# Expert slots filled by indirect gathers of stored token rows instead of one-hot products, with the shared products reordered

## The reference: what is computed

```python
x  = x + attn0(layernorm(x)) + ffn0(layernorm(x))      # 1024 tokens of 256
xn = layernorm(x)
x  = x + attn1(xn) + moe(xn)                           # attn1: 16 heads of 16, 4 key heads

def moe(x):                                            # E=32 experts, K=4, F=176, FS=704, CAP=32
    probs = softmax(x @ Wr)
    topw, topi = top_k(probs, 4); topw = topw / sum(topw)
    shared = silu(x @ Wsg) * (x @ Wsu) @ Wsd * sigmoid(x @ Wse)
    pos = number of earlier picks of the same expert   # valid if pos < CAP
    xe[sel, pos] += x[tok] * valid                     # 32 experts x 32 slots
    ye = (silu(xe @ Wg) * (xe @ Wu)) @ Wd
    return shared + sum over picks of ye[sel, pos] * w * valid
```

## Time and profile before

| what | value |
|---|---|
| median of 3 runs | 457.9 us (457.85 to 458.16) |
| the profiled execution | 458.18 us, of which 456.4 us are its span |
| TensorE busy | 439.0 us (96%) |
| VectorE busy | 301.4 us (66%) |
| ScalarE busy | 238.6 us (52%) |
| GpSimd busy | 157.5 us (35%) |
| granted clock of TensorE | 1.00 |

### The profile page before, as it was taken

How to read it: one execution, slowest core, us unless ns; L and a number is a source line. 1 busy time by engine, 2 the same in 40 slices (tenths; PEclk the granted TensorE clock), 3 DMA queues, 4 the chain that set the end, 5 groups by cost and what they waited for, 6 DMA issues and landing times.

```text
span 456.4 us, 8792 instructions
## 1 busy us (share of the span) xinstructions
PE 439.0 (96%) x3062; PEld 387.8 (85%) x3062; DVE 301.4 (66%) x889; ACT 238.6 (52%) x656; POOL 157.5 (35%) x286
## 2 busy tenths in 40 slices
PE   2999999999999999999999999999998999999997
PEld 1788888899999999999999999999986746568897
DVE  5735576678787878787877766486889952554111
ACT  3464561786868787878676883333161233242000
POOL 3050001545455555555555301011651289500000
PEclk9999999999999999999999999999999999999999
DMA  6910011401010101010000000000999099900011
GB/s 193 233 58 2 1 47 47 157 30 47 2 47 1 47 3 46 1 50 0 1 2 2 0 1 2 1 0 1 309 276 298 6 252 296 275 4 1 0 47 46
DMA packets 40442, 32.35 MB, mean 71 GB/s; under 512 B 6432, under 2 KB 38864, under 8 KB 40400
## 3 DMA queue, kind: packets, MB, share of 16 engines
q1 hardware_dynamic: 40400, 31.80, 25.2%
HBM read 30.75 MB, written 1.05 MB: 70 GB/s over the span
## 4 chain that ended last, share of the span: by engine, by line
PE 94%; DVE 2%; ACT 2%; issue 1%; DMA 1%; POOL 0%; DVEq 0%
PE bank L873 21%; PE bank L874 20%; PE bank L875 20%; PE bank L1252 5%; PE bank L1031 4%; PE bank L1183 3%; PE bank L1043 3%; PE bank L1022 3%; PE bank L1224 2%; PE bank L1291 2%; PE bank L1290 2%; PE bank L1288 2%; PE bank L1073 2%; PE bank L1244 1%; PE bank L1192 1%
## 5 line engine op out<-in xcount | busy, mean ns | idle before, releaser
L540 POOL TENSOR_TENSOR arena<-arena,rinv 128x384 f32<-128x384 f32 x64 | 52.9, 827 | 82.2 <-DVE rinv L1475 82.2
L873 PE MATMUL bank<-XTl,WA 128*128 128x512 f32 x128 | 54.2, 423 | 2.5 <-POOL WA L507 1.7
L874 PE MATMUL bank<-XTh,WA 128*128 128x512 f32 x128 | 51.3, 401 | 0.0
L875 PE MATMUL bank<-XTh,WA 128*128 128x512 f32 x128 | 51.2, 400 | 0.0
L708 ACT ACTIVATE PT<-bank 128x256 fp32r<-128x256 f32 x64 | 24.5, 382 | 34.1 <-PE bank L1031 34.1
L1479 DVE TENSOR_TENSOR PT<-bank,PT 128x256 fp32r<-128x256 f32 x64 | 27.2, 425 | 19.7 <-ACT arena L709 19.7
L873 PE MATMUL bank<-WA,XTh 128*128 128x256 f32 x128 | 38.4, 300 | 0.6 <-DVE K L1450 0.6
L874 PE MATMUL bank<-WA,XTl 128*128 128x256 f32 x128 | 35.7, 279 | 0.0
L875 PE MATMUL bank<-WA,XTh 128*128 128x256 f32 x128 | 35.7, 279 | 0.0
L531 POOL CAST Q<-arena 128x128 fp32r<-128x128 f32 x64 | 18.6, 290 | 48.0 <-PE bank L875 48.0
L701 ACT ACTIVATE arena<-arena,nmax 128x256 f32<-128x256 f32 x64 | 32.3, 505 | 0.0
(11 more groups left out here) (313 smaller groups left out, 1419.8 us busy)
## 6 DMA issues: line engine op xcount, KB each, us to landing
arena<-in_L_ffn_Wg SPq DMA_DIRECT2D x6, 704.0 KB, 8.6
arena<-in_L_ffn_Wu SPq DMA_DIRECT2D x6, 704.0 KB, 10.2
arena<-in_L_ffn_Wd SPq DMA_DIRECT2D x6, 512.0 KB, 8.4
arena<-in_L_attn_Wq SPq DMA_DIRECT2D x4, 512.0 KB, 6.3
arena<-in_L_attn_Wk SPq DMA_DIRECT2D x8, 256.0 KB, 2.6
arena<-in_L_attn_Wv SPq DMA_DIRECT2D x8, 256.0 KB, 3.1
arena<-in_L_attn_Wo SPq DMA_DIRECT2D x1, 2048.0 KB, 8.2
arena<-in_L_ffn_Wd SPq DMA_DIRECT2D x6, 192.0 KB, 7.7
```

What stands on the lines that cost most here:

```text
L540: pool.tensor_tensor(pr, pr, r[:, :, None].to_broadcast([P, 3, P]), ALU.mult).then_inc(s_p, 1)
L873: pe.matmul(dst, wh, xl, start=start, stop=False)
L874: pe.matmul(dst, wl, xh, start=False, stop=False)
L875: return pe.matmul(dst, wh, xh, start=False, stop=stop)
```

## The change

Slots are filled another way. SyncE stores each tile of `XN2` to a table `token_rows` in the chip's memory. The table of slots gives each slot its token number; VectorE writes it as an index, first of all that it makes of the table, and GpSimd issues eight indirect gathers, each of which brings 128 rows of 1 KB to their slots' partitions (a slot without a token gets row 0 and has weight 0). TensorE turns each group's rows (`slots_turn`, two transposes) and ScalarE copies them into `XE`, which has room for two groups. The one-hot masks stay, for `slot_table` alone. `XRh`, `XRl` and their steps go.

The order changes. Shared up 3 to 8 stand between the tables' products, ahead of the experts; 9 to 11 stand behind the table's turn. The shared-down tiles stand between the experts 4 to 6, and the first of the last products (`mix_first`, groups 0 to 5 of tiles 0 to 3) around expert 7. Attention's softmax moves behind the third and fourth expert group, and the chain on GpSimd with it. Shared down of tiles 4 to 7 and the projection become split products; ScalarE and VectorE make the parts (`parts`, `PJh`, `PJl`, `AOTh`, `AOTl`).

```diff
+EXPERT_STEPS = [("shared", (8, 1)), ("table", 0), ("shared", (9, 0)), ("shared", (9, 1)), ("shared", (10, 0)), ("shared", (10, 1)),
+                ("slots", 0), ("up", 0), ("shared", (11, 0)), ("shared", (11, 1)), ("slots", 1), ("up", 1), ("turn", 0),
+                ("slots", 2), ("down", 0), ("turn", 1), ("up", 2), ("down", 1), ("slots", 3), ("turn", 2), ("up", 3),
+                ("down", 2), ("turn", 3), ("slots", 4), ("down", 3), ("parts", 0), ("sd", 0), ("sd", 1),
...
+                ("up", 6), ("slots", 7), ("sd", 6), ("turn", 6), ("sd", 7), ("down", 6), ("mix", 0), ("mix", 1),
+                ("up", 7), ("mix", 2), ("turn", 7), ("mix", 3), ("down", 7)]
...
+            def store_rows(j):
+                sp.wait_ge(s_xn2, j + 1)
+                sp.dma_start(rows[P * j:P * j + P], XN2[:, j]).then_inc(s_xs, 16)
+
+            for j in range(NT - 2):
+                store_rows(j)
             sp.wait_ge(s_ol, 2 * NT)
...
+                if g == 0:
+                    store_rows(NT - 2)
...
-            products(6)
-            products(7)
-            pool.wait_ge(s_xr, 2)
-            pool.tensor_tensor(XRl[:, 4:8], XN2[:, 4:8], XRh[:, 4:8].bitcast(F32), ALU.subtract).then_inc(s_xrp, 1)
-            products(8)
-            pool.wait_ge(s_di, NT)
             pool.memset(WD[3][:, :, 1], 0.0).then_inc(s_pe, 1)
+            for n in range(6, 9):
+                products(n)
+            pool.wait_ge(s_xs, 16 * NT)
+            pool.wait_ge(s_ix, 1)
+            for g in range(GR):
+                pool.indirect_dma_start(XG[:, g], None, rows, bass.IndirectOffsetOnAxis(ap=idx[:, g:g + 1], axis=0)).then_inc(s_xg[g], 16)
+            pool.memset(ACTT[FC - 1][0:P - FT], 0.0).then_inc(s_ps, 1)
             pool.iota(IT, [[1, N]], base=0, channel_multiplier=0, allow_small_or_imprecise_dtypes=True).then_inc(s_it, 1)
...
+                    nc.scalar.activation(XE[:, n % 2], pb[1][:, 0:2 * P].rearrange("p (c n) -> p c n", c=C), ACT.Copy).then_inc(s_xe, 1)
...
+                if what == "parts":
+                    act.wait_ge(s_am, 1)
+                    nc.scalar.activation(SCf, SCf, ACT.Exp, scale=SCALE1).then_inc(s_ae, 1)
+                    act.wait_ge(s_sd, 32)
+                    act.wait_ge(s_ps, 2)
                     act.wait_ge(s_gl, FC)
+                    nc.scalar.activation(SDh[:], SD, ACT.Copy).then_inc(s_sdh, 1)
+                    act.wait_ge(s_sm, len(shared))
+                    for m in range(FC):
+                        nc.scalar.activation(ACTh[:, m], ACTT[m][:, N // 2:N], ACT.Copy).then_inc(s_adh, 1)
+                if what == "down" and n == 5:
...
-            def dispatch(j):
-                pe.wait_ge(s_dm, j + 1)
-                pe.wait_ge(s_xr, j // 4 + 1)
-                pe.wait_ge(s_xrp if j // 4 else s_xrl, 1)
-                for k in range(4):
-                    c, half = k // 2, k % 2
-                    for n, xr in enumerate((XRh, XRl)):
-                        pe.matmul(pb[4 + k][:], xr[:, j, P * c:P * c + P], DM[j % 4][:, 512 * half:512 * half + 512],
-                                  start=(j == 0 and n == 0), stop=(j == NT - 1 and n == 1))
-
             def slot_table(j):
                 if j == 0:
                     pe.wait_ge(s_wt, 1)
                     pe.wait_ge(s_wu, 1)
...
+            for q in (3, 4):
+                shared_up(q, 0)
+                shared_up(q, 1)
+            shared_up(5, 0)
+            slot_table(0)
+            slot_table(1)
+            shared_up(5, 1)
...
+            def slots_turn(g):
+                pe.wait_ge(s_xg[g], 16)
+                if g == 0:
+                    pe.wait_ge(s_sw1, 1)
+                    pe.wait_ge(s_sm, 9)
+                else:
+                    pe.wait_ge(s_xe, g)
+                for c in range(C):
+                    ins = pe.transpose(pb[1][:, P * c:P * c + P], XG[:, g, P * c:P * c + P], ident[:])
+                ins.then_inc(s_xtt, 1)
 
...
+                    if j < 4:
+                        ins = pe.matmul(pb[down_bank(j)][:, 0:D], ACTT[m][:, P * j:P * j + P], SD[:, m], start=(m == 0), stop=(m == FC - 1))
+                    else:
+                        ins = mm3(pb[down_bank(j)][:, 0:D], ACTh[:, m, ts], ACTl[m][:, ts], SDh[:, m], SDl[:, m], m == 0, m == FC - 1)
...
+            def mix_proj(j):
+                dst, ts = mix_tile(j)
+                for c in range(C):
+                    ins = mm3(dst, AOTh[:, c, ts], AOTl[:, c, ts], PJh[:, c], PJl[:, c], False, c == C - 1)
+                ins.then_inc(s_fo, 1)
...
+                if what == "parts":
+                    dve.wait_ge(s_ae, 1)
+                    step(nc.vector.tensor_reduce(mx1[:], SCf, AX, ALU.add))
+                    step(nc.vector.reciprocal(mx1[:], mx1[:]))
+                    nc.vector.tensor_tensor(SCf, SCf, mx1[:, :, None].to_broadcast([P, 128, 4]), ALU.mult).then_inc(s_ap, 1)
+                    dve.wait_ge(s_sdh, 1)
+                    nc.vector.tensor_tensor(SDl[:], SD, SDh[:].bitcast(F32), ALU.subtract).then_inc(s_sdl, 1)
+                    for m in range(FC):
+                        dve.wait_ge(s_adh, m + 1)
+                        nc.vector.tensor_tensor(ACTl[m][:], ACTT[m][:, N // 2:N], ACTh[:, m].bitcast(F32), ALU.subtract).then_inc(s_adl, 1)
+                if what == "sd" and n >= 1:
+                    add_shared(n - 1)
+                if what == "mix" and n == 0:
...
```

More of the change, by code:

```diff
@@ L1259, in _ @@
                     shared_up(*n)
+                if what == "slots":
+                    slots_turn(n)
                 if what == "up":
@@ L1265, in _ @@
                     expert_down(n)
-            pe.wait_ge(s_sd, 32)
-            pe.wait_ge(s_ps, 2)
-            pe.wait_ge(s_sm, len(shared))
-            for j in range(4):
-                shared_down(j)
+                if what == "sd":
+                    if n == 0:
+                        pe.wait_ge(s_sd, 32)
+                        pe.wait_ge(s_ps, 2)
+                        pe.wait_ge(s_sm, len(shared))
+                    shared_down(n)
+                if what == "mix":
+                    mix_first(n)
             pe.wait_ge(s_ye, GR)
@@ L1636, in _ @@
             dve.wait_ge(s_it, 1)
-            for j in range(3):
-                slots_of(j)
+            slots_of(0)
+            g_low(2)
             shared_product(1)
@@ L1664, in slot_weights @@
                 for h in range(2):
-                    table = pb[2 + h]
+                    ins = nc.vector.tensor_scalar(idx[:, 4 * h:4 * h + 4], pb[6 + h][:, 0:4 * TC].rearrange("p (g x) -> p g x", g=4)[:, :, 0],
+                                                  -1.0, 0.0, ALU.add, ALU.max)
+                ins.then_inc(s_ix, 1)
+                for h in range(2):
+                    table = pb[6 + h]
                     first = 1 + EPG * (GR // 2) * h
```

302 lines of the change are left out of this document (165 added, 137 removed).

## The result

The changed kernel takes 461.18 us, the median of 4 runs (460.59 to 462.1), where the kernel before beside it took 458.03 (4 runs). The ratio is 1.0067, with an interval of 1.005 to 1.0084: it is slower, by 3.1 us, against a forecast of 3.4 faster. The profiled execution took 461.18, of which 459.2 are its span. Before they were 458.18 and 456.4, so that the two traces differ by 2.8 to 3.0.

The account below looks back on a forecast made before the run. TensorE, busy 96% of the span, was taken as the bound: -18.7 us (work -16.1, holes -2.6), +9.1 for waits a to e and +6.2 for term f gave 454.5 us, range 449.5 to 462.

Parts of the forecast that it names:

- Work, -16.1: TensorE: dispatch products go (-14.9), split shared down (-1.8) and projection (-1.15) save, transposes add 1.75; 16.1 us less work.
- Term f: Expert turns 4 to 6: TensorE waits for VectorE's longer queue, slowed beside GpSimd's attention chain by 0.25 per step; 6.2 us.
- Rival B: Turns 4 to 6: full port locks, each VectorE step waits 0.65; 10.7 us there, 459.0 us in all; chance 0.08.
- a: Shared up (3,1) waits for VectorE's product 1, now behind a slot mask and a weight subtraction; +2.2 us.
- b: The table's turn waits for VectorE's copy of its half, which stands behind product 8; +1.5 us.
- c: Slots 0 and 1 go straight from transpose to ScalarE copy to up product, a SiLU ahead of the copy; +1.9 us.
- d: Smaller handovers in the expert stage: hidden of down 0, slot copy before up 3, down 3, a late mask; +1.7 us.
- e: Mix 0 waits for the last shared addition, +1.15 us; attention transposes wait for the last expert's copy, +0.7.
- Gathers: Eight indirect gathers on GpSimd, taken at 1.0 us each plus 1.7 to land; hidden behind TensorE's work, costing nothing.
- The margin before the padding: GpSimd's padding memset, needed by shared down 0, follows the gathers; each gather may take 2.4 us before it costs.
- Rival C: Gathers hold GpSimd 3.5 us each, so the padding memset ends 9.0 late at shared down 0; 463.5 us; chance 0.17.
- The softmax "at no cost": Softmax moved behind the experts is covered if the attention chain, starting near 391 us, ends before its transposes near 430.

Follow-up runs that it names:

- experiment 2: Changed kernel with TensorE making unread products in the holes, 20 before turn 4 and 40 before turn 6: 459.13 us (ratio to before 1.0016).
- experiment 1: Changed kernel with all 32 steps of GpSimd's attention chain on 16 of the 256 columns: 451.34 us (ratio to before 0.9834).
- experiment 7: Changed kernel with six small memsets, each waited for, behind each gather on GpSimd: 467.71 us (ratio to before 1.0187).
- Experiment 4: Changed kernel with attention's sums, maximum and softmax back ahead of the experts: 452.98 us (ratio to before 0.9885).
- best_plain: `best` with shared down of tiles 4 to 7 plain, without the steps on its parts: 447.73 us (ratio to before 0.9772).
- softmax_early: Changed kernel with attention's softmax back ahead of the experts, the run of Experiment 4: 452.98 us (ratio to before 0.9885).
- lows_late: Changed kernel with VectorE's six y_low steps behind the product that turn 6 waits for: 459.37 us (ratio to before 1.0032).
- held_gathers: Changed kernel with six memsets behind each gather on GpSimd, the run of experiment 7: 467.71 us (ratio to before 1.0187).
- narrow_chain: Changed kernel with GpSimd's attention chain on 16 of 256 columns, the run of experiment 1: 451.34 us (ratio to before 0.9834).
- best: Changed kernel with softmax early, experts' steps further apart, VectorE's product 1 and table copy earlier, last products reordered: 446.79 us (ratio to before 0.9741).
- experiments 5 and 6: Against the changed kernel: y_low later, 459.37 us, with softmax early 452.56; then softmax early with experts' steps further apart, 451.01, rerun 447.86.

## Why the prediction was wrong, step by step

- **Work, -16.1: TensorE's own steps were right, its clock was left out.** Where the granted clock stays up, work falls by 439.0 - 424.2 = 14.8. The last 1.3 I put down, without having shown it, to the ends of products that a hole no longer overlaps with the next. In the changed kernel work fell by 11.1: the other 3.7 are the lower clock behind the holes of 2.62 and 5.11 (with the holes filled, experiment 2, 3.0 of it were kept in the trace and 2.0 in the median). This is the first step that failed. The forecast itself put holes of 1.5 and 4 us before the turns 4 and 6, and then priced all that follows at the upper level. No row of before had such a hole, so none showed the price. The Trainium skill (TensorE: Matmul & The Clock Gate, "What's actually happening") has the two levels, the lower one after idling; these traces agree, with 0.21 against 0.119 for a product of 256 columns.
- **Term f, 6.2: measured 9.1, the second step that failed.** Where it would be was right, at the turns 4, 5 and 6: 2.6, 1.3 and 5.1 against 1.45, 0.8 and 3.95. Without contention I had 2.2; experiment 1 shows 2.1. What failed is "I take 0.25 per step, below both, since a GpSimd that is itself held up leaves gaps". The rows had 0.35 for a mask and 0.47 for a subtraction, and the runs show 0.32 to 0.40 and 0.44. The rows were right and the discount was not: put into the forecast's own working at their full size they give 3.0 + 1.2 + 4.65 = 8.9. (That working also takes 0.3 off at turn 4 and 0.2 at turn 5 without giving a reason.)
- **Rival B, 0.65 a step**, was too much a step, though its 10.7 for term f lies nearer the measured 9.1 than my 6.2 does. The Trainium skill (SBUF — State Buffer, "Who interferes with whom") has the shared pair of ports locked for a whole instruction, which rival B read as one GpSimd step of 0.65 for each step of VectorE. The traces show less, paid by both sides: VectorE 0.28 to 0.44, GpSimd 0.33 (a product 0.97 against 0.64) and 0.34 (an addition 1.06 against 0.72). The rule names the right pair of engines and operations, and too high a price here.
- **Terms a to e, 9.1: measured 7.2.** a 1.6 (2.2), b 1.5 (1.5), c 1.5 (1.9), d 1.2 (1.7, with the gather's 0.3), e 1.4 (1.85). These erred on the safe side, by 1.9.
- **Gathers:** 1.25 us each on GpSimd (forecast 1.0) and 2.9 to the first landing (1.7). The margin before the padding held in experiment 7. Rival C had no part in it.
- **The softmax "at no cost".** The forecast priced it as part of term f, but took the chain's late start as covered because TensorE's transposes were covered. The cover was the wrong one: the chain did end in time (422.4 against 439), and what it cost was VectorE's time on the way. Experiment 4 gives its price, 8.2 us.
- **The sum with the measured sizes:** -18.7 + 7.2 + 9.1 + 3.7 + 1.3 = +2.6, against 3.0 measured between the profiled executions. The rest lies before 342 us, where the changed kernel is 0.4 behind already.
- **The check named in the forecast,** "wrong if TensorE's idle time grows by over 16 us, or by under 8", did not show it: idle time grew by 13.9 while the time was wrong. The sign had no word on busy time.

## What to carry to other kernels

A hole on TensorE costs more than its length: if it lets the clock fall, the work behind it runs at half speed for a while (1.5 to 2.7 us lost a time here), so a forecast that adds holes must add that too, and an order with the same holes made shorter gains twice. Before a long chain on GpSimd is moved, list the two-input and wide VectorE steps that it will lie beside, and price each at what the trace shows for such a pair, without a discount. Such a change is worth its new machinery only with an order to match: the same gathers and splits lose 0.7% in one order and gain 2.6% in another.

## What the runs showed of the hardware

- In the profiled executions the clock fell behind holes of 1.87, 2.15, 2.62, 3.0 to 3.1, 5.1 to 5.2 and 6.13 us. It stayed up behind one of 1.92 in `best_plain`, 2.13 in `softmax_early`, 2.31 in `lows_late` and 2.80 in `held_gathers`, and behind all of 1.6 or less. The length of the hole alone does not decide it; and of one kernel (`narrow_chain`, `softmax_early`, `best`) some executions had a mean granted clock of 1.000 and others 0.996.
- Filling a hole with products that nobody reads made the kernel faster, by 2.0 us in the median and 3.0 in the trace.
- An indirect gather of 128 rows of 1 KB occupied GpSimd for 0.95 us (the first 1.14), came every 1.25, and landed 2.9 us after its issue when little else moved. Over the eight of the changed kernel the median was 4.2 and the longest 6.9; the last ones ran beside the loads of the experts' weights.
- ScalarE's start 1.5 us late (experiments 5 and 6) came and went with the same program; between the two runs of that kernel it made 3.1 us. Its cause is open.
